# A gated-slot attention kernel: the next unit's scan and reciprocal moved ahead on VectorE, three quantisation steps moved behind the multiplications by the gate

## The chip, the cores and the metric

The kernel runs on one core of one Trainium2 chip. The metric is the device time of one execution in microseconds (us). TensorE is called PE, VectorE DVE, ScalarE ACT, GpSimd POOL and SyncE SP, as the profile calls them.

## What is computed

Four sequences of 512 tokens with 512 features pass a layer of gated slot attention with 16 heads and then a gated feed-forward layer whose weights are rounded to an 8-bit floating-point format. Cut to what the change touches:

```
q, k, v, s, g = LN(x) @ (Wq, Wk, Wv, Ws, Wg)      # per head: 64, 64, 128, 64, 128 wide
z = cumlogsumexp(clip(s, -32, 32)) over tokens    # gate g_t = exp(z[t-1]-z[t]), p = exp(s-z)
hk = hk*g_t + k_t p_t ;  ok = q_t . hk            # scan over tokens
pv = softmax(ok)
hv = hv*g_t + p_t v_t ;  ov = pv . hv             # scan over tokens
o  = ov * rsqrt(mean(ov^2)+eps) * g_norm * silu(g)
x  = x + o @ Wo
x  = x + down(silu(gate(LN(x))) * up(LN(x)))      # weights quantised to fp8
```

In the kernel e is exp(clip(s)), and the running sum of e over the tokens, inverted, is called c: the scan and the reciprocal of the change's name compute it. Both products with hk and hv are done in four chunks of 128 tokens with masked score matrices.

## The kernel before, in words

Work is cut into 32 units: 8 pairs of heads, and in each pair the 4 sequences. A unit u runs the attention of one pair on one sequence; while it does, PE also makes the projections of unit u+1 (`nu`, `ni` in the code). These projections are seven jobs in the order ST (slot logits s), KTJ (k), QT (q) and VG0 to VG3 (v and g of one chunk of 128 tokens each), of twelve 512-column multiplications each, since every operand is split in a high and a low part. The jobs write two PSUM banks in turn, so a job starts only when the job two before it has been drained: VG3 waits for VG1's bank, and ST, the first job of the unit after, waits for VG2's (`job` and `wait_drained`, L371 to L411).

A VG job is drained by two engines. ACT copies v out and takes tanh of half of g (L656, L660); DVE then forms (tanh+1)*g in `gate(c, u, i)` (L885 to L890), and its semaphore `s_g` is what PE waits for. The tanh tile is single: ACT's next tanh waits for DVE's gate on the one before.

Units 0 to 28 are written as one unit and a loop over seven pairs of four units; the last three units are the tail, in which the layer norm of the feed-forward layer is begun (`norm_tokens`, `norm_lo`, and on PE `norm_transposes`, L566 to L574). In the units before the tail DVE also rounds one slice of the feed-forward weights in eight steps (`quantise`, L990 to L1009); SP loads a slice into the tile q8 and stores it when the eighth step is done.

There is no scheduler: the order on each engine is the order in which `unit` of that engine's block is written, and semaphores join the engines. The change is in `unit` of the DVE block (L1011 to L1086), from L1066 on. There, for unit u, DVE goes through:

- `gate(0)` of the next unit; `mask_value_weights(u)` (L901), for which PE's product at L544 waits; `mask_scores(nu)` (L892)
- in the tail `norm_tokens` of two tiles; then `gate(1)` of the next unit
- the last three quantisation steps, L1001 to L1003 (not in the tail)
- `times_gate(u, i, 1)` (L938), `sums(nu, ni)` (L877: a scan at L880, a reciprocal at L883), `times_gate(u, i, 0)`
- in the tail `norm_lo` and `norm_tokens` of the other tiles; then `gate(2)` and `gate(3)` of the next unit

On PE the same stretch holds, in order: the product of masked weights and values (L544), in the tail two tiles' transposes, the jobs VG2 and VG3, in the tail two more tiles' transposes, then in the next unit the transposes of k (L448) and of e (L453), and its job ST. `sums` itself waits only for the exponentials of the next unit (`s_e`), and its result is first read in the next unit at L1034.

Of the kernel before, what the change touches and what calls it, by code (L numbers as in the profile page):

```python
# [145 lines left out]
def attention(nc, sb_top, sem, x, Wq, Wk, Wv, Wg, Ws, Wo, gnorm, flat, gate_s, up_s, fp8_scratch, shared):  # L146
# [3 lines left out]
    with ExitStack() as ctx:  # L150
# [101 lines left out]
        def job_bank(j, i):  # L252

            at = HEAD_JOBS.index(j) if i == 0 else STEADY_JOBS.index(j)
            return PJ[(JOBS * i + at) % 2]
# [603 lines left out]
        def _(dve):  # L859
# [5 lines left out]
            def lo_vg(pair, k):  # L865

                dve.wait_ge(s_vgh, pair * KT + k + 1)
                lo(vgl[:, k, :], stage_vg[:, k, :], vgh[:, k, :]).then_inc(s_vgl, 1)

            def clip(u, i):  # L870
                dve.wait_ge(s_job, job_count(ST, u, i))
                if not isinstance(u, int) or u >= 2:
                    dve.wait_ge(s_b, u - 1)
                dve.tensor_scalar(eT[i % 2][:, :], job_bank(ST, i)[:, :], -CLAMP, CLAMP,  # L874
                                  ALU.max, ALU.min).then_inc(s_clip, 1)

            def sums(u, i):  # L877

                dve.wait_ge(s_e, u + 1)
                dve.tensor_tensor_scan(cT[i % 2][:, :], eT[i % 2][:, :], eT[i % 2][:, :], 0.0, ALU.add,  # L880
                                       ALU.bypass).then_inc(s_scan, 1)
                dve.wait_ge(s_scan, u + 1)
                dve.reciprocal(cT[i % 2][:, :], cT[i % 2][:, :]).then_inc(s_cinv, 1)  # L883

            def gate(c, u, i):  # L885

                dve.wait_ge(s_th, u * CH + c + 1)
                dve.scalar_tensor_tensor(out=g[i % 2][:, c, :, :].rearrange("p a d -> p (a d)"), in0=th[:, :], scalar=1.0,  # L888
                                         in1=job_bank(VGS[c], i)[:, 2 * DV:4 * DV],
                                         op0=ALU.add, op1=ALU.mult).then_inc(s_g, 1)  # L890
# [18 lines left out]
            def key_states(u):  # L909

                dve.wait_ge(s_hkd, u + 1)
                if not (isinstance(u, int) and u == 0):
                    dve.wait_ge(s_ok, u)
                for a in range(2):
                    rows, cols = slice(64 * a, 64 * (a + 1)), slice(M * a, M * (a + 1))
                    dve.tensor_copy(hk[rows, :, cols],
                                    O[0][rows, 0:(CH - 1) * M].rearrange("p (s m) -> p s m", m=M)).then_inc(s_hk, 1)
# [14 lines left out]
            def mean_square(u):  # L932
                dve.wait_ge(s_sq, 8 * (u + 1))
                dve.wait_ge(s_es, u + 1)
                dve.scalar_tensor_tensor(out=ssq[:, :], in0=ssq[:, :], scalar=1.0 / DV, in1=es[:, :],  # L935
                                         op0=ALU.mult, op1=ALU.add).then_inc(s_ms, 1)

            def times_gate(u, i, a):  # L938

                if a:  # L940
                    dve.wait_ge(s_o, 2 * (u + 1))
                    if not (isinstance(u, int) and u == 0):
                        dve.wait_ge(s_tro, 2 * u)
                else:
                    dve.wait_ge(s_sq, 8 * u + CH)
                dve.tensor_tensor(o[:, a, :, :], O[a][:, :].rearrange("p (c d) -> p c d", c=CH),
                                  g[i % 2][:, :, a, :], ALU.mult).then_inc(s_oev, 1)

            def out_norm(u):
                dve.wait_ge(s_rstd, u + 1)  # L950
                dve.wait_ge(s_oev, 2 * (u + 1))
                for a in range(2):
                    scale = rstd[:, :].rearrange("p (c a) -> p c a", a=2)[:, :, a:a + 1].broadcast_to([P, CH, DV])
                    dve.tensor_tensor(o[:, a, :, :], o[:, a, :, :], scale, ALU.mult).then_inc(s_og, 1)

            def out_lo(u, banks):
                for a in range(2):
                    dve.wait_ge(s_oh, 2 * u + a + 1)
                    lo(ol[:, a, :], banks[a][:, :], oh[:, a, :]).then_inc(s_ol, 1)
# [22 lines left out]
            def norm_lo(b, tiles):  # L982
                for c in tiles:
                    t = CH * b + c
                    dve.wait_ge(s_nh, t + 1)
                    cols = slice(t * P, (t + 1) * P)
                    lo(xl[:, :, cols], A[c % 2][:, :].rearrange("p (k t) -> p k t", k=KT), xh[:, :, cols]
                       ).then_inc(s_nl, 1)
# [22 lines left out]
            def unit(u, i, last=False, tail=False):  # L1011
                first = isinstance(u, int) and u == 0
                nu, ni = u + 1, i + 1
                if tail and i >= 2:
                    norm_lo(i - 2, (2, 3))
                if not first:
                    mean_square(u - 1)
                if not last:
                    clip(nu, ni)
                if not first:  # L1020
                    out_norm(u - 1)
                key_states(u)
                value_states(u)
                if not first:
                    out_lo(u - 1, A)
                if i == 3 and not tail:
                    for k in range(2):
                        lo_vg(h_of[0] + 1, k)

                dve.wait_ge(s_ok, u + 1)  # L1030
                dve.wait_ge(s_cinv, u + 1)
                if not first:
                    dve.wait_ge(s_trw, u)
                dve.scalar_tensor_tensor(out=p[:, :].rearrange("p (n t) -> p n t", n=2), in0=ok_both, scalar=SCALE,  # L1034
                                         in1=cT[i % 2][:, :].rearrange("p (n t) -> p n t", n=2),
                                         op0=ALU.mult, op1=ALU.mult).then_inc(s_oks, 1)
                if not first:
                    add_y(u - 1, i - 1, 0)
                    add_y(u - 1, i - 1, 1)

                p3, ok3 = (s[:, :].rearrange("p (s m) -> p s m", m=M) for s in (p, T0))
                dve.wait_ge(s_trs, u + 1)
                dve.tensor_reduce(mx[:, :], ok3, AX.X, ALU.max).then_inc(s_max, 1)
                dve.wait_ge(s_max, u + 1)
                dve.tensor_tensor(p3, ok3, mx[:, :].rearrange("p (s a) -> p s a", a=1).broadcast_to([P, 2 * CH, M]),  # L1045
                                  ALU.subtract).then_inc(s_sub, 1)
                if not first:
                    add_y(u - 1, i - 1, 2)
                    add_y(u - 1, i - 1, 3)
                dve.wait_ge(s_exp, u + 1)  # L1050
                dve.tensor_reduce(sm[:, :], p3, AX.X, ALU.add).then_inc(s_sum, 1)
                if tail:
                    norm_statistics(i - 1)
                else:
                    quantise(u, slice(0, 2))
                dve.wait_ge(s_sum, u + 1)
                dve.scalar_tensor_tensor(out=es[:, :], in0=sm[:, :], scalar=EPS, in1=sm[:, :],
                                         op0=ALU.mult, op1=ALU.mult).then_inc(s_es, 1)

                dve.wait_ge(s_trw, u + 1)  # L1060
                if not first:
                    dve.wait_ge(s_oi, u)
                dve.tensor_tensor(wT[:, :], T1[:, :], cT[i % 2][:, :], ALU.mult).then_inc(s_wT, 1)
                if not tail:
                    quantise(u, slice(2, 5))
                if not last:  # L1066
                    gate(0, nu, ni)
                mask_value_weights(u, i)
                if not last:
                    mask_scores(nu, ni)  # L1070
                if tail:
                    norm_tokens(i - 1, (0, 1))
                if not last:
                    gate(1, nu, ni)
                if not tail:
                    quantise(u, slice(5, Q8_STEPS))
                times_gate(u, i, 1)
                if not last:
                    sums(nu, ni)
                times_gate(u, i, 0)  # L1080
                if tail:
                    norm_lo(i - 1, (0, 1))
                    norm_tokens(i - 1, (2, 3))
                if not last:
                    gate(2, nu, ni)
                    gate(3, nu, ni)  # L1086
# [295 lines left out]
```

## Time and profile before

| what | us |
|---|---|
| median of three runs | 1505.59 |
| lowest and highest run | 1503.77, 1508.01 |
| the profiled execution, its own time | 1505.37 |
| its span, first to last instruction | 1503.7 |
| PE busy | 1431.0 (95%) |
| DVE busy | 1006.4 (67%) |
| ACT busy | 433.3 (29%) |
| POOL busy | 144.3 (10%) |

The profile is of one execution. A unit takes about 36.7 us, the head ends at some 42 us, the attention units at some 1217 us, and the feed-forward layer takes the rest. The granted TensorE clock is 0.992 of full speed in the mean. Busy times of PE overlap at their ends: a 512-column multiplication is shown as 0.39 us long though the next begins 0.23 us after it.

### The profile page before, as it was taken

The page shows a single profiled execution, that of the slowest core. Times are in us where ns is not written, and L with a number is a line of the kernel's source. Part 1 is how long each engine was busy: PE and PEld are TensorE (multiplying, and loading weights), DVE is VectorE, ACT ScalarE, POOL GpSimd, SP SyncE. Part 2 cuts the span into 40 slices and gives each one's busy share as a digit, 9 for nine tenths or more (in the row PEclk, how much of TensorE's full clock was granted, in tenths as well). Part 3 has the DMA queues.
Part 4 walks back from the last instruction along what each step waited for, and adds up shares of the span by engine and source line. Part 5 has one row for each costly group of instructions (what it writes and reads, how often), then busy time and mean ns, then how long its engine had stood idle before and what let it go on. Part 6 is the DMA issues. An engine that isn't in the chain of part 4 may idle for free. (4 is left out here: it accounts for less than half of the span.)

```text
span 1503.7 us, 23604 instructions
## 1 busy us (share of the span) xinstructions
PE 1431.0 (95%) x8480; PEld 1172.0 (78%) x8480; DVE 1006.4 (67%) x1619; ACT 433.3 (29%) x1243; POOL 144.3 (10%) x106
## 2 busy tenths in 40 slices
PE   7899999999999999999999999999999879999998
PEld 6777777777777787778777878787777758888886
DVE  8677776777677777776767776767677764535354
ACT  4323332333223323332323232323232222222221
POOL 3001110111011101110101110111010000000000
PEclk9999999999999999999999999999999989999999
DMA  5011002101110101020102100210000113000000
GB/s 168 20 58 39 22 23 62 39 18 37 42 39 18 50 29 39 18 60 25 32 18 60 31 26 18 61 32 25 18 17 1 57 57 146 29 0 28 0 29 28
DMA packets 61019, 57.23 MB, mean 38 GB/s; under 512 B 7297, under 2 KB 50049, under 8 KB 60929
## 3 DMA queue, kind: packets, MB, share of 16 engines
q1 hardware_dynamic: 60928, 55.87, 11.9%
q8 instruction: 76, 1.25, 0.4%
q14 instruction: 15, 0.11, 0.0%
HBM read 42.22 MB, written 13.63 MB: 37 GB/s over the span
## 5 line engine op out<-in xcount | busy, mean ns | idle before, releaser
L360 PE MATMUL bank<-wvg_hi,xT_hi 128*128 128x512 f32 x512 | 208.8, 408 | 0.0
L362 PE MATMUL bank<-wvg_hi,xT_lo 128*128 128x512 f32 x512 | 200.5, 392 | 0.0
L361 PE MATMUL bank<-wvg_lo,xT_hi 128*128 128x512 f32 x512 | 200.1, 391 | 0.0
L613 ACT ACTIVATE a_and_v<-bank 128x256 f32<-128x256 f32 x128 | 49.0, 383 | 294.4 <-PE bank L362 294.4
L964 DVE TENSOR_TENSOR y<-y,bank 128x512 f32<-128x512 f32 x128 | 87.7, 685 | 66.0 <-PE bank L362 65.8
L888 DVE SCALAR_TENSOR_TENSOR g<-tanh_half_g,bank 128x256 f32<-128x256 f32 x128 | 53.3, 417 | 94.2 <-ACT tanh_half_g L660 94.2
L832 POOL TENSOR_TENSOR rstd<-ssq,neg_half 128x8 f32<-128x8 f32 x32 | 52.4, 1636 | 656.3 <-DVE ssq L935 656.3
L360 PEld LDWEIGHTS bank<-wvg_hi,xT_hi 128*128 128x128 f32 x512 | 96.5, 188 | 21.3 <-issue 0.4
L362 PEld LDWEIGHTS bank<-wvg_hi,xT_lo 128*128 128x128 f32 x512 | 96.2, 188 | 20.8
L361 PEld LDWEIGHTS bank<-wvg_lo,xT_hi 128*128 128x128 f32 x512 | 96.6, 189 | 17.4
L360 PE MATMUL bank<-wo_hi,oT_hi 128*128 128x512 f32 x256 | 107.0, 418 | 1.5 <-DVE oT_lo L863 1.5
L883 DVE RECIPROCAL cT<-cT 128x512 f32<-128x512 f32 x32 | 107.3, 3353 | 1.1
L362 PE MATMUL bank<-wo_hi,oT_lo 128*128 128x512 f32 x256 | 101.3, 396 | 0.0
L361 PE MATMUL bank<-wo_lo,oT_hi 128*128 128x512 f32 x256 | 100.3, 392 | 0.0
L1306 DVE SCALAR_TENSOR_TENSOR gated<-tanh_half,bank 128x512 f32<-128x512 f32 x48 | 32.9, 686 | 100.3 <-ACT tanh_half L1274 100.3
L360 PE MATMUL bank<-xT_hi,ws_hi 128*128 128x512 f32 x128 | 55.0, 430 | 36.8 <-issue 24.9
L1260 PE MATMUL bank<-w_down,fuse_hi 128*128 128x512 f32 x192 | 75.6, 394 | 0.1
L1260 PE MATMUL bank<-w_down,fuse_lo 128*128 128x512 f32 x192 | 75.4, 393 | 0.0
L874 DVE TENSOR_SCALAR eT<-bank 128x512 f32<-128x512 f32 x32 | 22.1, 692 | 71.7 <-PE bank L362 71.7
L1274 ACT ACTIVATE tanh_half<-bank,gate_scale 128x512 f32<-128x512 f32 x48 | 33.1, 689 | 120.8 <-PE bank L119 108.6
L718 ACT ACTIVATE p<-p 128x512 f32<-128x512 f32 x32 | 20.3, 633 | 152.7 <-DVE p L1045 152.7
L544 PEld LDWEIGHTS bank<-a_and_v 128*128 128x128 f32 x512 | 62.1, 192 | 2.7
(157 smaller groups left out, 3215.5 us busy)
## 6 DMA issues: line engine op xcount, KB each, us to landing
fp_weights<-q SPq DMA_DIRECT2D x28, 318.0 KB, 2.6
stage_vg<-in_L_attn_Wv SPq DMA_DIRECT2D x32, 128.0 KB, 2.7
stage_vg<-in_L_attn_Wg SPq DMA_DIRECT2D x32, 128.0 KB, 3.2
stage<-in_L_attn_Wo SPq DMA_DIRECT2D x16, 256.0 KB, 2.7
out<-result SPq DMA_DIRECT2D x16, 256.0 KB, 2.1
y<-in_L_attn_hidden_states SPq DMA_DIRECT2D x3, 1024.0 KB, 9.0
w_down<-fp_weights SPq DMA_DIRECT2D x3, 1024.0 KB, 12.0
q<-in_L_ffn_gate_w SPq DMA_DIRECT2D x28, 106.0 KB, 2.0
```

What stands on the lines that cost most here:

```text
L360: pe.matmul(dst, w_hi, m_hi, start=(k == 0), stop=False)
L361: pe.matmul(dst, w_hi, m_lo, start=False, stop=False)
L362: last = pe.matmul(dst, w_lo, m_hi, start=False, stop=(k == n - 1))
L544: mm = pe.matmul(O[a][:, c * P:(c + 1) * P], av[par][:, a, c, 0, :], av[par][:, a, c, 1, :], start=False, stop=(c == CH - 1), skip_group_c ...
L613: return act.activation(dst, src, ACT.Copy)
L832: pool.tensor_tensor(rstd[:, :], ssq[:, :], neg_half[:, :], ALU.pow).then_inc(s_rstd, 1)
L883: dve.reciprocal(cT[i % 2][:, :], cT[i % 2][:, :]).then_inc(s_cinv, 1)
L888: dve.scalar_tensor_tensor(out=g[i % 2][:, c, :, :].rearrange("p a d -> p (a d)"), in0=th[:, :], scalar=1.0, in1=job_bank(VGS[c], i)[:, 2 ...
L964: dve.tensor_tensor(y[:, t, :], y[:, t, :], out_bank(u, c)[:, :], ALU.add).then_inc(s_ya, 1)
L1260: mm = pe.matmul(Y[c][:, :], part[:, f % 2, c * P:(c + 1) * P], wd[:, f, :], start=(f == 0 and part is fh), stop=(f == FT - 1 and part is fl))
L1274: act.activation(th[:, f % 2, :], gate_up_bank(bank, f, 0)[:, :], ACT.Tanh, scale=hgs[:, f:f + 1]).then_inc(s_th, 1)
L1306: dve.scalar_tensor_tensor(out=ga[:, f % 2, :], in0=th[:, f % 2, :], scalar=1.0, in1=gate_up_bank(bank, f, 0)[:, :], op0=ALU.add, op1=ALU.mult
```

## The change

In DVE's unit, `sums` of the next unit now stands directly in front of `gate(1)`, and the two `times_gate` stand directly behind that gate, ahead of the last three quantisation steps. No instruction is added or removed, and no other engine's order changes.

```diff
                 if tail:
                     norm_tokens(i - 1, (0, 1))
                 if not last:
+                    sums(nu, ni)
                     gate(1, nu, ni)
+                times_gate(u, i, 1)
+                times_gate(u, i, 0)
                 if not tail:
                     quantise(u, slice(5, Q8_STEPS))
-                times_gate(u, i, 1)
-                if not last:
-                    sums(nu, ni)
-                times_gate(u, i, 0)
                 if tail:
                     norm_lo(i - 1, (0, 1))
                     norm_tokens(i - 1, (2, 3))
```

On DVE, in unit 0, from the second of the two masked scores (L898) to the gates of VG2 and VG3; the loop's units have the same order with register instructions between. L888 is `gate`, L1001 to L1003 the last quantisation steps, L946 `times_gate`, L880 and L883 scan and reciprocal. Before:

```order
L898 TENSOR_TENSOR a_and_v<-bank,tri 128x4x128
L888 SCALAR_TENSOR_TENSOR g<-tanh_half_g,bank 128x256 [waits tanh_ready]
L1001 TENSOR_SCALAR q8t<-q8t 128x3x208 [waits fp8_step]
L1002 TENSOR_SCALAR q8t<-q8t 128x3x208 [waits fp8_step]
L1003 SCALAR_TENSOR_TENSOR q<-q8t,q 128x3x208 [waits fp8_step]
L946 TENSOR_TENSOR o<-bank,g 128x512 [waits o_done]
L880 SCALAR_TENSOR_TENSOR cT<-eT 128x512 [waits e_ready]
L883 RECIPROCAL cT<-cT 128x512 [waits c_summed]
L946 TENSOR_TENSOR o<-bank,g 128x512 [waits o_squared]
L888 SCALAR_TENSOR_TENSOR g<-tanh_half_g,bank 128x256 [waits tanh_ready] x2
```

With the change:

```order
L898 TENSOR_TENSOR a_and_v<-bank,tri 128x4x128
L880 SCALAR_TENSOR_TENSOR cT<-eT 128x512 [waits e_ready]
L883 RECIPROCAL cT<-cT 128x512 [waits c_summed]
L888 SCALAR_TENSOR_TENSOR g<-tanh_half_g,bank 128x256 [waits tanh_ready]
L946 TENSOR_TENSOR o<-bank,g 128x512 [waits o_done]
L946 TENSOR_TENSOR o<-bank,g 128x512 [waits o_squared]
L1001 TENSOR_SCALAR q8t<-q8t 128x3x208 [waits fp8_step]
L1002 TENSOR_SCALAR q8t<-q8t 128x3x208 [waits fp8_step]
L1003 SCALAR_TENSOR_TENSOR q<-q8t,q 128x3x208 [waits fp8_step]
L888 SCALAR_TENSOR_TENSOR g<-tanh_half_g,bank 128x256 [waits tanh_ready] x2
```

Scan and reciprocal have moved ahead of the gate of VG1 and of three quantisation steps; the gate of VG2 still follows the same eight instructions.

On DVE in the tail, in unit 30 (unit 29 reads the same but for one wait fewer), from the second `norm_tokens` tile (L979) on; L863 is `norm_lo`. Before:

```order
L979 TENSOR_SCALAR q8t<-y,q8t 128x512 [waits n_transposed]
L888 SCALAR_TENSOR_TENSOR g<-tanh_half_g,bank 128x256 [waits tanh_ready]
L946 TENSOR_TENSOR o<-bank,g 128x512 [waits o_transposed,o_done]
L880 SCALAR_TENSOR_TENSOR cT<-eT 128x512 [waits e_ready]
L883 RECIPROCAL cT<-cT 128x512 [waits c_summed]
L946 TENSOR_TENSOR o<-bank,g 128x512 [waits o_squared]
L863 TENSOR_TENSOR xT_lo<-bank,xT_hi 128x4x128 [waits nT_hi_ready] x2
L979 TENSOR_SCALAR q<-y,q8t 128x512 [waits n_transposed,ln_sd_ready]
L979 TENSOR_SCALAR q8t<-y,q8t 128x512 [waits n_transposed]
```

With the change:

```order
L979 TENSOR_SCALAR q8t<-y,q8t 128x512 [waits n_transposed]
L880 SCALAR_TENSOR_TENSOR cT<-eT 128x512 [waits e_ready]
L883 RECIPROCAL cT<-cT 128x512 [waits c_summed]
L888 SCALAR_TENSOR_TENSOR g<-tanh_half_g,bank 128x256 [waits tanh_ready]
L946 TENSOR_TENSOR o<-bank,g 128x512 [waits o_transposed,o_done]
L946 TENSOR_TENSOR o<-bank,g 128x512 [waits o_squared]
L863 TENSOR_TENSOR xT_lo<-bank,xT_hi 128x4x128 [waits nT_hi_ready] x2
L979 TENSOR_SCALAR q<-y,q8t 128x512 [waits n_transposed,ln_sd_ready]
L979 TENSOR_SCALAR q8t<-y,q8t 128x512 [waits n_transposed]
```

Here too scan and reciprocal stand in front of the gate of VG1; what follows them keeps its order.

## Rows read from the trace of the kernel before

**Rows 1.** The page's busy times of each engine.

```profile
PE 1431.0 (95%) x8480; PEld 1172.0 (78%) x8480; DVE 1006.4 (67%) x1619; ACT 433.3 (29%) x1243; POOL 144.3 (10%) x106
```

**Rows 2.** Groups by form, PE: line, engine, names, shapes, count, busy, mean, idle before.

```profile
L360 PE MATMUL bank<-xT_hi,ws_hi 128*128 128x512 f32 x128 | 55.0, 430 | 36.8 <-issue 24.9 <-DVE g L888 10.3 <-DVE xT_lo L863 1.5
```

**Rows 3.** Timeline of PE, end of unit 12: start, us, engine, line, names, [idle before].

```profile
516.14 0.39 PE L360 MATMUL bank<-wvg_hi,xT_hi 128*128 128x512 f32 x1
...
519.19 0.60 PE L453 MATMUL bank<-ident,eT 128*128 128x128 f32 x4
521.22 0.48 PE L360 MATMUL bank<-xT_hi,ws_hi 128*128 128x512 f32 x1 [1.43 <-issue]
...
524.18 0.88 PE L466 MATMUL bank<-e_tok,k_tok_then_wT 128*64 128x192 f32 x12
```

**Rows 4.** Timeline of DVE, the same stretch.

```profile
509.00 1.27 DVE L898 TENSOR_TENSOR a_and_v<-bank,tri 128x512 f32<-128x512 f32 x2
512.61 0.42 DVE L888 SCALAR_TENSOR_TENSOR g<-tanh_half_g,bank 128x256 f32<-128x256 f32 x1 [2.34 <-ACT tanh_half_g L660]
512.95 0.79 DVE L1001 TENSOR_SCALAR q8t<-q8t 128x636 f32<-128x636 f32 x1
...
515.04 0.68 DVE L946 TENSOR_TENSOR o<-bank,g 128x512 f32<-128x512 f32 x1
515.64 1.22 DVE L880 TENSOR_TENSOR_SCAN cT<-eT 128x512 f32<-128x512 f32 x1
516.89 3.35 DVE L883 RECIPROCAL cT<-cT 128x512 f32<-128x512 f32 x1
520.16 0.63 DVE L946 TENSOR_TENSOR o<-bank,g 128x512 f32<-128x512 f32 x1
520.71 0.41 DVE L888 SCALAR_TENSOR_TENSOR g<-tanh_half_g,bank 128x256 f32<-128x256 f32 x1
```

**Rows 5.** Timeline of ACT, the same stretch: tanh of VG2.

```profile
516.62 0.38 ACT L660 ACTIVATE tanh_half_g<-bank 128x256 f32<-128x256 f32 x1
```

**Rows 6.** Timeline of PE, tail, unit 29.

```profile
1143.54 0.39 PE L362 MATMUL bank<-wvg_hi,xT_lo 128*128 128x512 f32 x1
1145.18 0.63 PE L572 MATMUL bank<-ident,q 128*128 128x128 f32 x4 [1.26 <-DVE q L979]
...
1146.41 0.60 PE L453 MATMUL bank<-ident,eT 128*128 128x128 f32 x4
1146.77 0.48 PE L360 MATMUL bank<-xT_hi,ws_hi 128*128 128x512 f32 x1
```

**Rows 7.** Timeline of DVE, tail, unit 29.

```profile
1134.57 0.54 DVE L979 TENSOR_SCALAR q8t<-y,q8t 128x512 f32<-128x512 f32 x1
...
1143.31 1.27 DVE L863 TENSOR_TENSOR xT_lo<-bank,xT_hi 128x512 fp32r<-128x512 f32 x2
```

**Rows 8.** A stretch at the end of unit 8: busy time of each engine, granted clock (PEclk), DMA.

```profile
373.00:376.00 3.00, 2.77 (x9) 2.26 (x10) 0.71 (x3) 1.36 (x3) 1.60 (x1) 0.73 0.79 216
```

**Rows 9.** Timeline of PE: ST behind units 8 and 24, L466 behind unit 8.

```profile
373.23 0.47 PE L360 MATMUL bank<-xT_hi,ws_hi 128*128 128x512 f32 x1 [1.94 <-issue]
...
377.62 0.95 PE L466 MATMUL bank<-e_tok,k_tok_then_wT 128*64 128x192 f32 x12
...
961.94 0.47 PE L360 MATMUL bank<-xT_hi,ws_hi 128*128 128x512 f32 x1 [2.24 <-issue]
```

**Rows 10.** Single lines, durations in ns min/median/max: reciprocal; one quantisation step.

```profile
L883 DVE RECIPROCAL cT<-cT x32: 3353/3353/3353, 42.1 to 1178.0; 128x512 f32<-128x512 f32 x32
...
L1000 DVE TENSOR_TENSOR q8t<-q x29: 809/821/1781, 66.3 to 1093.0; 128x636 f32<-128x636 f32 x28, 128x624 f32<-128x624 f32 x1
```

**Rows 11.** Timeline of POOL, the same stretch as rows 3 to 5.

```profile
512.12 1.28 POOL L793 TENSOR_TENSOR wo_lo<-stage,wo_hi 128x512 fp32r<-128x512 f32 x1 [5.25 <-ACT wo_hi L613]
```

**Rows 12.** Timeline of DVE, unit 13: its first quantisation step.

```profile
538.28 0.48 DVE L996 TENSOR_SCALAR q8t<-q 128x636 int32<-128x636 int32 x1
```

**Rows 13.** The page's DMA issues: names, queue, count, KB, us to landing.

```profile
fp_weights<-q SPq DMA_DIRECT2D x28, 318.0 KB, 2.6
```

## The prediction

> **What bounds the kernel now.** I read the page's busy times first: PE works 1431.0 of 1503.7 us, DVE 1006.4 [rows 1]. So DVE's work as such is free, and the change can only act through places where PE stands still. The second view groups PE's instructions by form and gives the idle time in front of each. One group holds half of all that is missing: 36.8 us in front of the job ST, of which 1.5 us lie in the head [rows 2]. The other 35.3 us are 29 waits of 0.7 to 2.2 us, one behind each of the units 0 to 28; I take that count from the timeline, where rows 3 and 9 show three of them. The profile puts most of them down to "issue", so the third step is to see in the timelines what they end with. ST starts at 521.22 [rows 3]. ST needs VG2's bank, which is free when DVE's gate of VG2 is done: that gate runs from 520.71 for 0.41, to 521.12 [rows 4]. The wait ends 0.10 us behind it. So the gate of VG2 is what PE waits for, and the question is what keeps it: its tanh was ready at 516.62 + 0.38 = 517.00 [rows 5]. DVE came 3.7 us later, because it had worked without a break since 512.61. Before that it had stood still for 2.34 us, waiting for the tanh of VG1 [rows 4]. The reader is to see both: an idle stretch, then a queue that runs late, on an engine that is idle a third of the time.
>
> **The scan and the reciprocal.** They need only the exponentials of the next unit, which that unit's ACT work made early in unit 12, long before. They can run in the idle stretch. On DVE an instruction starts about 0.08 us before the end shown for the one ahead, so I take start-to-start times [rows 4]: scan 516.89 - 515.64 = 1.25, reciprocal 520.16 - 516.89 = 3.27, gate 512.95 - 512.61 = 0.34, first multiplication by the gate 515.64 - 515.04 = 0.60, second 520.71 - 520.16 = 0.55, three quantisation steps 515.04 - 512.95 = 2.09. The masked scores end at 509.00 + 1.27 = 510.27, so in the new order: scan 510.19, reciprocal 511.44, gate of VG1 at 514.71 to 515.13. That is 2.1 us later than before. Who waits for this gate? ACT's tanh of VG2, not due before 516.62 [rows 5], and PE's job VG3, which starts at 516.14 [rows 3]. A margin of 1.0 us is left, and it is the narrowest place of the change. The move costs nothing while this holds.
>
> **The two multiplications.** They follow at 515.05 and 515.65. The first needs PE's product L544 and ran at 515.04 before, without idle time ahead of it [rows 4], so it is where it was. The second needs the squares of head 0 too, which ACT makes directly behind L544, and before it tanh of VG2 at 516.62 [rows 5]; should they come as late as that, the multiplication would slip by 1 us, and the gate of VG2 by 0.2 us past its margin below. I take no slip. ACT's squares of head 1 need the first alone.
>
> **The quantisation steps.** They run at 516.20, 517.03 and 517.56, to 518.29. What they feed is SP's store of the slice and, through it, the load of the next one. It was finished at about 515.1, now 518.4, 3.3 us later. The store lands 2.6 us after issue [rows 13]; the three loads of 106 KB are smaller than that store, so I bound them by another 2.6. That makes some 523.6, against 538.28 for the first step that reads them [rows 12], or 536.6 once the unit is shorter. The other loads in SP's queue behind this store are bounded by the same shift, and feed splits a unit later. Cover of 13 us: cost zero. If it were gone, each us over it would delay DVE's L1063 and with it PE.
>
> **The gate of VG2, and the gain.** It follows at 518.29 and ends at 518.71. PE could take ST as soon as the transposes of e are issued. What that would be without a wait is seen in the tail: transposes at 1146.41, ST at 1146.77, 0.36 us on [rows 6]. In unit 12: 519.19 + 0.36 = 519.55. The gate is 0.8 us ahead of that. So the wait goes wholly, and 521.22 - 519.55 = 1.67 us are won here. This is 0.24 more than the 1.43 shown as idle, since the profile's ends of pipelined multiplications overlap. For all 29: 35.3 + 29 x 0.24 = **42.3 us**. The waits longer than the usual (2.24 us behind unit 24 [rows 9]) come from a later tanh of VG1, and the new order covers that too: the tanh may come 2.1 us later than in unit 12 before it matters.
>
> **What is late next.** Once ST starts earlier, the stretch from ST to the next unit's masked scores moves with it, since DVE's clip, the transposes and all else there hang on PE. Beside it run the tanh of VG3 and ACT's copies of k and e, which L466 needs 2.96 us after ST [rows 3]. The tanh of VG3 waited for the gate of VG2 too, so it moves up with it. I find nothing that stays behind, and price this at zero, with the first rival for the case that something does.
>
> **The tail.** In units 29 and 30 there is no quantisation. The second norm tile of L979 ends at 1134.57 + 0.54 = 1135.11; scan, reciprocal, gate and two multiplications give 1135.03, 1136.28, 1139.55, 1139.89, 1140.49, then `norm_lo` at 1141.04. It ran at 1143.31 [rows 7]; it lasts 1.27 - 0.08 = 1.19, and the norm tile for which PE waited ends at 1142.23 + 0.54 = 1142.77. PE reaches L572 about 0.22 us after the start of VG3's last multiplication, at 1143.76, and waited until 1145.18 [rows 6]. Won: 1.4 us, in two units **2.8 us**. Unit 31 has neither scan nor quantisation and stays.
>
> **The clock.** Behind unit 8, after PE's wait of 1.94 us, the granted clock is 0.73 in the mean [rows 8], so part of the job ran at 1.2 GHz; ST to L466 took 377.62 - 373.23 = 4.39 us [rows 9] against 2.96 behind unit 12. The longer wait behind unit 24 had no such fall. Without these waits I expect no fall in the units, and take **1.4 us** for it; the bounds are 0 (another place falls instead) and 1.4. The Trainium skill's "TensorE: Matmul & The Clock Gate", section "Part 1: The HAM clock gate", says that the clock is halved unless the engine is kept busy, and that where the change falls varies from run to run; the trace agrees as far as one of 29 waits goes.
>
> **A price beside POOL.** In unit 12 POOL works from 512.12 to 513.40 [rows 11], where the first quantisation step took 0.79; an L1000 took 1.781 us at most against 0.821 in the middle [rows 10], so DVE can be slowed. In the new order the reciprocal lies there, in every fourth unit. It was 3.353 all 32 times [rows 10], but I cannot tell from the trace whether it ever ran beside such work. Bounds: 0 and the 0.96 us of L1000. With 0.96 the gate of VG1 ends 1.0 us before VG3 less 0.96, still in time, and the gate of VG2 comes 0.2 us late in 8 units: 1.6 us. I take 0, as the reciprocal reads one tensor. The skill's "VectorE: DVE Perf Modes", section "Two Vector instructions with no wait between them", says that the read path shared with GpSimd is the one that a second input or a 2-port mode uses; by it the reciprocal is free of POOL, and the sum would be the same 0 where L1000's row alone would give 1.6.
>
> **The sum.** 42.3 + 2.8 + 1.4 = 46.5 us off the profiled execution's 1505.4: **1458.9 us**. That execution stands 0.2 us under the median of the runs, so this is a median too. About 0.3% of 1505, 4.5 us, is what a measurement can tell from no change.
>
> **Rivals.**
> - A new wait takes part of it. PE arrives 1.7 us earlier at L466 and at the output transposes, and the chain gate of VG3, mean square, POOL's power, normalisation might be what then ends last. For it: this chain runs over three engines. Against: its first link moves up with the tanh. If half of the 42.3 is given back, 1458.9 + 21 = 1480 us. 11 in 100.
> - The change does not reach the wait. If "issue" were the sequencer's own time, as the label says for most of it, ST would start when it did: 1505 us. Against: the end of the gate and ST's start lie 0.10 us apart. 4 in 100.
> - Slower: the gate of VG1 becomes VG3's wait. Its place is the first multiplication of VG3. It bites once the gate ends over 1.0 us later than I work out, and outweighs the 1.45 us won per unit from 2.45 us on. If the reciprocal took twice its time in its new place, 3.35 more, VG3 would be 2.4 us late, and 29 x (2.4 - 1.45) = 28 us would be lost: 1533 us. Against: 32 equal durations. With smaller mishaps of the same kind, 5 in 100.
> - The forecast: 80 in 100. Its own range is 1456 (tail and clock give 2 to 3 us more) to 1463 (no gain from the clock, POOL's 1.6, a pair of small waits).
>
> **How the numbers follow.** The range goes up into the first rival, to a fourth or a third given back, 1473, and 1 us under the forecast's own low end, 1455. Faster by over 0.3%: the forecast and the first rival, 0.91. Within 0.3%: the second, 0.04. Slower: 0.05.
>
> **What would show it.** In the profile after: in the group of ST, idle near zero but for the head's 1.5; on DVE no idle before the gate of VG1, which starts where the reciprocal ends, about 3.1 us after the start of L544; gate of VG2 ended before PE's transposes of e are through; VG3 still without a wait; units of 35.3 us instead of 36.7; L572 in the tail without its 1.26. The granted clock stays at 1.00 in the units. The prediction is wrong if PE's idle time turns up before L466, L431 or VG3, or if the waits before ST stay.

## The result, and the profile after

The changed kernel takes 1460.63 us (median of four runs, 1458.88 to 1463.23) against 1504.72 us before. The ratio is 0.9705, with a 95% interval of 0.9683 to 0.9726: 3% faster, by some 44 us. The prediction was 1458.9 us. The profiled execution is the slowest of the four, 1463.23 us with a span of 1461.5; the profiled one of before took 1505.37 with a span of 1503.7.

First the page's busy times after, which answer to [rows 1]; then the group of ST's first multiplications by form, which answers to [rows 2].

```profile
PE 1424.2 (97%) x8480; PEld 1171.4 (80%) x8480; DVE 1001.0 (68%) x1619; ACT 430.3 (29%) x1243; POOL 145.2 (10%) x106
```

```profile
L360 PE MATMUL bank<-xT_hi,ws_hi 128*128 128x512 f32 x128 | 54.0, 422 | 1.5 <-DVE xT_lo L863 1.5
```

The 36.8 us in front of ST have become 1.5, which are those of the head. The timeline shows how, at the end of the same unit 12, which began its L544 (the product of masked weights and values) at 493.30 here and at 511.62 before. DVE, after (before: [rows 4]):

```profile
491.85 1.21 DVE L880 TENSOR_TENSOR_SCAN cT<-eT 128x512 f32<-128x512 f32 x1
493.09 3.35 DVE L883 RECIPROCAL cT<-cT 128x512 f32<-128x512 f32 x1
496.36 0.36 DVE L888 SCALAR_TENSOR_TENSOR g<-tanh_half_g,bank 128x256 f32<-128x256 f32 x1
496.64 1.27 DVE L946 TENSOR_TENSOR o<-bank,g 128x512 f32<-128x512 f32 x2
497.83 0.48 DVE L1001 TENSOR_SCALAR q8t<-q8t 128x636 f32<-128x636 f32 x1
...
499.61 0.41 DVE L888 SCALAR_TENSOR_TENSOR g<-tanh_half_g,bank 128x256 f32<-128x256 f32 x1
501.42 0.42 DVE L888 SCALAR_TENSOR_TENSOR g<-tanh_half_g,bank 128x256 f32<-128x256 f32 x1 [1.40 <-ACT tanh_half_g L660]
```

And PE, after, in the same stretch (before: [rows 3]):

```profile
493.30 1.95 PE L544 MATMUL bank<-a_and_v 128*128 128x128 f32 x16
...
497.81 0.39 PE L360 MATMUL bank<-wvg_hi,xT_hi 128*128 128x512 f32 x1
...
500.92 0.60 PE L453 MATMUL bank<-ident,eT 128*128 128x128 f32 x4
501.27 0.48 PE L360 MATMUL bank<-xT_hi,ws_hi 128*128 128x512 f32 x1
```

No idle time stands in front of the gate of VG1 any more. It starts 3.06 us behind the start of L544 and ends at 496.72, 1.09 us ahead of VG3, which starts at 497.81. The gate of VG2 ends at 500.02, and ST follows the transposes of e after 0.35 us without a wait. DVE's idle time has moved to the gate of VG3, where nobody is kept by it.

In the tail the waits of 1.26 us are gone. These are the second pairs of transposes in units 29 and 30 (before: [rows 6]); the third wait of the kind, in unit 31, stays, as forecast:

```profile
1100.95 0.60 PE L572 MATMUL bank<-ident,q 128*128 128x128 f32 x4
...
1138.03 0.60 PE L572 MATMUL bank<-ident,q 128*128 128x128 f32 x4
...
1171.46 0.63 PE L572 MATMUL bank<-ident,q 128*128 128x128 f32 x4 [0.42 <-DVE q L979]
```

What did not come as forecast is the clock in the tail. Three stretches of it, with busy times of PE, PEld, DVE, ACT and POOL, granted clock, DMA share and GB/s:

```profile
1144.00:1149.00 5.00, 4.07 (x15) 3.64 (x16) 3.98 (x9) 1.19 (x2) 0.06 (x1) 0.66 0.32 119
...
1162.00:1166.00 4.00, 4.00 (x25) 3.32 (x22) 2.20 (x4) 0.00 (x0) 0.00 (x0) 0.57 0.00 0
...
1177.00:1184.00 7.00, 6.49 (x18) 5.20 (x19) 2.13 (x4) 0.00 (x0) 0.00 (x0) 0.60 0.01 4
```

The first two places, the output product of L477 and L431 and the last unit's scores, ran at full clock before; the third was at half clock before too:

```profile
1190.00:1195.00 5.00, 4.40 (x26) 3.84 (x27) 4.42 (x10) 1.14 (x2) 0.00 (x0) 1.00 0.02 5
...
1205.00:1209.00 4.00, 3.73 (x37) 3.26 (x38) 2.42 (x5) 0.00 (x0) 0.64 (x1) 1.00 0.00 0
...
1217.00:1224.00 7.00, 5.11 (x16) 4.09 (x17) 2.54 (x5) 1.19 (x2) 0.00 (x0) 0.54 0.00 1
```

### The profile page after: what moved, and what is told of

Read it like the earlier page. It is cut to its first block and busy times, and to the rows that moved or that the text cites. A ratio compares the mean times of both kernels' runs of the same rounds, so it can differ in the third digit from the quotient of the medians.

```text
span 1461.5 us, 23604 instructions
## 1 busy us (share of the span) xinstructions
PE 1424.2 (97%) x8480; PEld 1171.4 (80%) x8480; DVE 1001.0 (68%) x1619; ACT 430.3 (29%) x1243; POOL 145.2 (10%) x106
## 5 line engine op out<-in xcount | busy, mean ns | idle before, releaser
L361 PE MATMUL bank<-wvg_lo,xT_hi 128*128 128x512 f32 x512 | 200.0, 391 | 0.0
L361 PEld LDWEIGHTS bank<-wvg_lo,xT_hi 128*128 128x128 f32 x512 | 96.5, 189 | 17.3
L883 DVE RECIPROCAL cT<-cT 128x512 f32<-128x512 f32 x32 | 107.3, 3353 | 1.1
L361 PE MATMUL bank<-wo_lo,oT_hi 128*128 128x512 f32 x256 | 100.8, 394 | 0.0
L888 DVE SCALAR_TENSOR_TENSOR g<-tanh_half_g,bank 128x256 f32<-128x256 f32 x128 | 51.6, 403 | 52.5 <-ACT tanh_half_g L660 52.5
L544 PEld LDWEIGHTS bank<-a_and_v 128*128 128x128 f32 x512 | 62.1, 192 | 2.7
L544 PE MATMUL bank<-a_and_v 128*128 128x128 f32 x512 | 62.3, 275 | 0.0
```

The lines of the kernel that those rows point to most:

```text
L361: pe.matmul(dst, w_hi, m_lo, start=False, stop=False)
L544: mm = pe.matmul(O[a][:, c * P:(c + 1) * P], av[par][:, a, c, 0, :], av[par][:, a, c, 1, :], start=False, stop=(c == CH - 1), skip_group_c ...
```

## The experiments

The kernel before was measured again beside each group of experiments, on the same chip, and each ratio is to that time. Its median was 1506.33 us beside the first three and the first of the faster versions, 1507.26 beside the two with added work, and 1506.93 beside the changed kernel's repeat, the one on the loop's head and the second of the faster versions.

### Which of the two moves wins: scan and reciprocal alone

```diff
                 if not last:
                     sums(nu, ni)
                     gate(1, nu, ni)
-                times_gate(u, i, 1)
-                times_gate(u, i, 0)
                 if not tail:
                     quantise(u, slice(5, Q8_STEPS))
+                times_gate(u, i, 1)
+                times_gate(u, i, 0)
```

(against the changed kernel)

> Only the scan and the reciprocal are moved ahead of the gate of VG1; the three quantisation steps stay between that gate and the multiplications. My theory (PE waits for the end of the gate of VG2, and it moves up because scan and reciprocal fill DVE's idle time): the gate of VG2 follows the same eight instructions, so the time is that of the whole change, 1460.6 us within 3. Rival (the multiplications by the gate had to come earlier, or the steps had to move): less of the gain, 1470 us or more, with idle time in front of ST.

Measured: 1462.37 us, ratio to before 0.9702 [0.9682, 0.9722]. The changed kernel, measured again, took 1462.39 us, ratio 0.9704 [0.9688, 0.9720]. The group of ST has the same 1.5 us. So moving scan and reciprocal is the whole gain, and moving the quantisation steps on top of it changes nothing.

### The quantisation steps alone

```diff
                 if not last:
                     gate(1, nu, ni)
-                if not tail:
-                    quantise(u, slice(5, Q8_STEPS))
                 times_gate(u, i, 1)
                 if not last:
                     sums(nu, ni)
                 times_gate(u, i, 0)
+                if not tail:
+                    quantise(u, slice(5, Q8_STEPS))
```

(against the kernel before)

> Only the three quantisation steps are moved, behind the two multiplications; scan and reciprocal stay between these. My theory: the gate of VG2 still ends behind all eight instructions, which start after the idle time, so nothing is won: 1504.7 us within 3, and 35 us of idle time in front of ST. Rival (the order of steps and multiplications carries part of the gain): under 1495 us.

Measured: 1529.54 us, ratio 1.0157 [1.0134, 1.0180], 23 us slower than before; I had expected no change. Groups by form of this kernel, PE and DVE:

```profile
L360 PE MATMUL bank<-xT_hi,ws_hi 128*128 128x512 f32 x128 | 56.4, 441 | 55.3 <-issue 37.7 <-DVE g L888 16.1 <-DVE xT_lo L863 1.5
```

```profile
L946 DVE TENSOR_TENSOR o<-bank,g 128x512 f32<-128x512 f32 x64 | 42.2, 661 | 20.0 <-PE bank L544 19.9
```

The expectation left out that the first multiplication by the gate needs PE's L544. The steps used to fill that time. Without them DVE reaches the multiplication 0.67 us too early in most units and stands still, 20.0 us in all, where the group has 3.6 us in the kernel before. The gate of VG2 is later by that much: 55.3 us in front of ST instead of 36.8. The rest of the 23 us goes with the clock, which fell in five of the units (512-column multiplications of 0.63 us, from 80.4, 305.7, 606.3, 756.5 and 981.7 on) and in one (unit 8) in the kernel before, behind waits that now last 1.9 to 2.0 us at these five places. So the second half of the change would be a loss without the first. With it the multiplications come 1.4 us after L544's results, and the steps need not fill anything.

### Only the end of the gate of VG2

```diff
                 if not last:
                     gate(1, nu, ni)
-                if not tail:
-                    quantise(u, slice(5, Q8_STEPS))
                 times_gate(u, i, 1)
...
                 if not last:
                     gate(2, nu, ni)
                     gate(3, nu, ni)
+                if not tail:
+                    quantise(u, slice(5, Q8_STEPS))
```

(against the kernel before)

> The order of before, but the three quantisation steps stand behind the gate of VG3, so the gate of VG2 ends 1.8 us earlier though scan and reciprocal stay where they were. My theory (only the end of the gate of VG2 counts): it ends before PE's transposes are through (7.3 against 7.9 us behind the start of L544), so nearly all of the gain appears: 1461 to 1468 us, the upper end if the mean square, 1.8 us later, makes the output transposes wait. Rival (the gain needs the scan in DVE's idle time): about 1504 us.

Measured: 1471.56 us, ratio 0.9767 [0.9747, 0.9788]: 34.8 us faster, 3.6 above the upper end of what I expected. Scan and reciprocal are where they were, and yet four fifths of the gain are there, so it is the end of the gate of VG2 that counts and not the place of the scan. The missing fifth, 9.2 us against the 1462.37 of scan and reciprocal alone, has three parts in the traces. The first is the same L544: DVE waits 21.8 us for it here, so that the gate of VG2 starts 7.65 us behind the start of L544 and ends at 8.06, where I had expected 7.3, just past PE's 7.93. ST starts at 8.16, in seven units at 8.43: 22 x 0.23 + 7 x 0.50 = 8.6 us. The second is the tail, where scan and reciprocal stand in their old place and both waits of 1.26 us are back: from unit 29's L544 to unit 31's pass 73.4 us here and 70.5 with scan and reciprocal alone, 2.9 us. The third goes the other way: with scan and reciprocal alone PE loses 3.1 us that it does not lose here, 2.2 at the loop's head and 0.9 in front of unit 0's VG3 (both are taken up below). From unit 0's L544 to unit 29's it is therefore 1029.9 against 1024.2 us, 5.7 more, and with the tail 8.6. In the view of groups the 8.6 us in front of ST hardly show; of the 3.3, 1.5 are the head's:

```profile
L360 PE MATMUL bank<-xT_hi,ws_hi 128*128 128x512 f32 x128 | 54.2, 423 | 3.3 <-issue 1.8 <-DVE xT_lo L863 1.5
```

The 0.24 us per wait that the overlapped ends hide are the larger part here: 6.8 of 8.6 us.

### The margin: more work in front of the gate of VG1

```diff
                     sums(nu, ni)
+                    dve.reciprocal(pad[:, 0:N], eT[ni % 2][:, 0:N])
                     gate(1, nu, ni)
```

(against the changed kernel, with N = 96 and N = 384; `pad` is a new tile that nobody reads)

> The whole change, and in front of the gate of VG1 one more reciprocal on DVE, of 96 columns into a tile that nobody reads: some 0.65 us by the 3.35 us of 512 columns. My theory of the margin: the gate of VG1 ends 1.0 us and the gate of VG2 1.1 us before PE needs them, so the addition is free: 1461 us within 3. Rival (DVE bounds the unit in the new order): 31 x 0.65 = 20 us more, 1481 us.

> The same with a reciprocal of 384 columns, about 2.45 us from start to start. My theory: the gate of VG1 now ends 1.45 us behind the moment at which PE could start VG3, in each of 31 units, and the gate of VG2 just before its own: 45 us more, about 1506 us, and the idle time stands in front of VG3, not of ST. Rival one (DVE bounds): 31 x 2.45 = 76 us more, 1537 us. Rival two (PE's queue hides it): under 1475 us.

Measured: 1465.73 us with 96 columns (ratio 0.9729 [0.9713, 0.9745]) and 1517.13 us with 384 (1.0073 [1.0056, 1.0090]). Who waited for whom on PE, of the kernel with 384 columns (us in total, times, longest; its lines are one higher, so L361 is the first line of `product3`, L449 the transposes of k, L889 the gate):

```profile
PE bank L361 <- DVE g L889: 40.0, 31, 2.0
...
PE bank L449 <- issue: 5.9, 6, 1.1
```

The forecast wait is there, 31 times, once per unit, at one place:

```profile
523.29 0.47 PE L361 MATMUL bank<-wvg_hi,xT_hi 128*128 128x512 f32 x1 [1.31 <-DVE g L889]
```

1.31 us shown plus what overlap hides is about the 1.45 us expected: a unit inside a pass of the loop lasts 36.7 us from L544 to L544, where the changed kernel takes 35.21, so 1.5 us; 31 of them are 46. ST has no wait. This turns the rival "the gate of VG1 becomes VG3's wait" into something seen: it bites from about 1 us of added work (2.45 us added less the 1.5 lost), and with 2.45 us added the kernel is slower than the one before. The total is 11 us above what I expected. Most of it stands in the units from L544 to L544. The six that reach over a jump back of the loop are 1.1 to 1.4 us longer than the others, 7.7 us in all, where the changed kernel's repeat has 1.9. The first lasts 39.0 us, with half clock from 78.6 on. The changed kernel itself takes 1.8 us more in its repeat than the 1460.6 from which I worked. The 1465.73 us with 96 columns are 1.7 above the range that I gave. The gate makes no wait in the loop, only one of 1.1 us in unit 0, but the row of L449 is there too:

```profile
PE bank L449 <- issue: 4.7, 6, 1.0
...
PE bank L361 <- DVE g L889: 1.1, 1, 1.1
```

So 0.7 us more on DVE costs nothing in front of VG3 and ST in the steady units. What the kernel has over the changed one, 3.3 us, lies mostly elsewhere: at the first instruction of the loop's body PE stood still in six of seven passes, each time that it had jumped back.

### The loop's head

In the changed kernel PE's transposes of k also wait at the loop's head, 0.7 us in three of seven passes, and in the kernel before 0.28 once. In the kernel with 96 columns SP's store of the quantised slice is issued at 220.90, 0.96 us ahead of such a wait at 221.86.

```diff
-                if not tail:
-                    quantise(u, slice(5, Q8_STEPS))
...
                 if not last:
                     gate(2, nu, ni)
                     gate(3, nu, ni)
+                if not tail:
+                    quantise(u, slice(5, Q8_STEPS))
```

(against the kernel with 96 columns added)

> The kernel with the added reciprocal of 96 columns showed PE idle at the first instruction of the loop's body (the transposes of k), in six of the seven passes, 4.7 us in all, put down to issue. There SP's store of the quantised slice starts 1 us ahead of that instruction. Here the last three quantisation steps stand behind the gate of VG3, so that the store starts 3 us later, behind the loop's head; one more reciprocal stays. Theory (the store's transfer delays PE's first instruction after the jump back): that idle time goes, under 1 us is left, and the time is 1461 to 1466 us, the rest from the mean square coming later. Rival (the longer program delays it, wherever the store lies): 4 to 5 us of idle time stay there.

Measured: 1466.82 us, ratio 0.9736 [0.9720, 0.9752]. The row that decides, who waited for whom on PE:

```profile
PE bank L449 <- issue: 3.8, 6, 0.9
```

The store is now issued at 223.63, 2.2 us behind the instruction that waited at 221.44, and the wait stays. My theory of the store is refuted.

The traces say more. Each has an instruction queue (q8, kind "instruction") beside the data queue, and at every jump back one 16 KB packet of it lands shortly before PE's transposes of k. It is this one in the kernel with 96 columns, behind unit 8, where L449 starts at 363.86 after 0.98 us of idle time (queue, kind: packets, MB, share, window 361.0 to 362.5):

```profile
q8 instruction: 1, 0.02, 3.9%
```

It ran from 361.37 to 362.29, and L449 started 1.6 us behind its end. All eleven traces together have 66 jumps back. In the 38 where PE is shown idle there, the transposes start 1.51 to 1.62 us behind the end of the packet, though the packets last from 0.9 to 1.8 us; in the 28 others they start 1.52 to 2.01 us behind it, never sooner. And the packet's own start follows the gate of VG1, for which PE waits last ahead of the jump, in front of VG3:

| kernel | gate of VG1 ends | packet starts | PE idle shown at the head |
|---|---|---|---|
| before | 1.3 to 2.2 | 4.3 | 0.28 us, once |
| changed | 3.4 | 4.7 to 5.0 | 0.7 us |
| with 96 columns | 4.0 | 5.3 to 5.9 | 4.7 us |
| with 384 columns | 5.85 | 7.1 to 7.6 | 5.9 us |

(us behind the start of L544, over the six jumps back of each trace.) In the eight kernels in which scan and reciprocal stand ahead of that gate the packet starts 1.3 us behind the gate's end in 36 of 48 cases, and up to 1.9 us in the others; the two kernels with added work move the gate and the packet moves with it. So the reading that fits all 66 is that PE waits at the loop's head for instructions, and that these are fetched later when the gate of VG1 ends later. It is a second place, besides VG3, where that gate costs time, and at the changed kernel's 3.4 us its margin is already used up. No kernel without the jump was run, and why the packet starts 0.5 us later in some cases is not shown.

### A faster version: three more waits of the same kind

```diff
-            sums(0, 0)
             dve.wait_ge(s_const, 4)
             mask_scores(0, 0)
             gate(B - 1, 0, 0)
+            sums(0, 0)
...
+                if not first:
+                    mean_square(u - 1)
                 if tail and i >= 2:
                     norm_lo(i - 2, (2, 3))
-                if not first:
-                    mean_square(u - 1)
...
-                if tail:
+                if tail and not last:
                     norm_statistics(i - 1)
-                else:
+                elif not tail:
                     quantise(u, slice(0, 2))
...
                 dve.tensor_tensor(wT[:, :], T1[:, :], cT[i % 2][:, :], ALU.mult).then_inc(s_wT, 1)
+                if last:
+                    norm_statistics(i - 1)
```

(against the changed kernel)

> The whole change and three more reorderings on DVE: in the head the scan and the reciprocal behind the masked scores and the gate of VG3; in the tail the mean square ahead of the leftover norm tiles; in the last unit the layer-norm statistics behind L1063. Each takes work from in front of something PE waits for: 3.3 us (L448 in the head), 2.0 us (L431 in unit 31) and 2.75 us (L527 in unit 31). My theory, that each wait ends with the DVE instruction named and nothing else is as late: 8 us off 1460.6, 1452.6 us, up to 3 us less where a fall of the clock behind a wait goes too. Rival: the next wait is as late, and under 3 us are won.

> The kernel with the three reorderings in head and tail, and of the change only the scan and reciprocal moved (the quantisation steps again ahead of the multiplications by the gate), so the store starts 1.2 us earlier, at 5.2 instead of 6.4 us behind the start of L544. My theory: the same time, 1452.3 us within 2. Rival (the place of the quantisation steps matters by itself): over 1455 us.

Measured: 1452.30 us, ratio to before 0.9636 [0.9620, 0.9653], and with the quantisation steps back between the gate of VG1 and the multiplications 1451.61 us, ratio 0.9633 [0.9617, 0.9649]. The second was measured beside the changed kernel's 1462.39: 10.8 us less. Who waited for whom on PE, changed kernel first:

```profile
PE bank L431 <- DVE o L954: 4.2, 2, 2.3
PE bank L448 <- DVE a_and_v L898: 3.3, 1, 3.3
PE bank L527 <- DVE k_tok_then_wT L1063: 2.8, 1, 2.8
```

and the version with all three:

```profile
PE bank L431 <- DVE o L954: 2.3, 1, 2.3
...
PE bank L448 <- DVE a_and_v L898: 0.9, 1, 0.9
```

Two waits are gone; of the head's 3.3 us 0.9 stay. That makes 7.1 of the 10.8 us. Most of the rest is the clock, in two places. Unit 0's L544 starts at 66.80 us in the second version and at 70.24 in the changed kernel's repeat, 3.4 us sooner where 2.4 of the wait went: the half clock there (0.50 from 46 to 49 us in the changed kernel) is gone. The nine other traces all have it, and neither of these two. From unit 30's L544 to unit 31's 28.7 us pass instead of 35.0, 6.3 less where 4.7 of waits went: a stretch at half clock is gone there too. This one cannot be credited to the reordering alone, since the kernel with scan and reciprocal alone has the same waits and no fall there. The two versions, which differ by the place of the quantisation steps alone, agree within 0.7 us, as the first experiment did.

## Why the prediction was right

**What bounds.** The reading held: the idle time in front of ST ended with the gate of VG2, though the profile calls most of it "issue". The experiment on the end of that gate shows it, since another way to bring it forward also wins.

**The gain in the units.** From unit 0's L544 to unit 29's the kernel before takes 1135.65 - 70.55 = 1065.10 us, the changed one 1092.84 - 70.27 = 1022.57. L544 of units 0, 29, 30 and 31, before:

```profile
70.55 1.95 PE L544 MATMUL bank<-a_and_v 128*128 128x128 f32 x16
...
1135.65 1.95 PE L544 MATMUL bank<-a_and_v 128*128 128x128 f32 x16
...
1174.14 1.95 PE L544 MATMUL bank<-a_and_v 128*128 128x128 f32 x16
...
1208.99 1.95 PE L544 MATMUL bank<-a_and_v 128*128 128x128 f32 x16
```

and after:

```profile
70.27 1.95 PE L544 MATMUL bank<-a_and_v 128*128 128x128 f32 x16
...
1092.84 1.95 PE L544 MATMUL bank<-a_and_v 128*128 128x128 f32 x16
...
1129.91 1.95 PE L544 MATMUL bank<-a_and_v 128*128 128x128 f32 x16
...
1166.39 1.95 PE L544 MATMUL bank<-a_and_v 128*128 128x128 f32 x16
```

That is 42.5 us won against 42.3 + 1.4 = 43.7 forecast for waits and clock together. The missing 1.2 us stand at the loop's head. In the changed kernel 24 of the 29 stretches from L544 to L544 last 35.21 us; the five others, 0.1 to 0.5 us longer and 1.4 in all, are each one that reaches over a jump back. Before, such a delay stood there twice (0.4 and 0.1 us), hidden behind the wait for the gate of VG2; the change lets it show, and lengthens it by ending the gate of VG1 later. I had no term for it: "the move costs nothing while this holds" and "I find nothing that stays behind" were wrong by 1.2 us.

**Margins.** The forecast start of the gate of VG1, 3.09 us behind L544's start, came at 3.06. Its margin of 1.0 us was 1.09 in unit 12, and the two kernels with added work show where it ends. But unit 12 is not the narrowest place. In unit 0 the gate of VG1 starts 3.71 us behind L544 and ends 0.45 us ahead of VG3, and in the repeat of the same kernel it is late:

```profile
69.42 1.29 POOL L793 TENSOR_TENSOR wo_lo<-stage,wo_hi 128x512 fp32r<-128x512 f32 x1 [4.12 <-ACT wo_hi L613]
69.46 2.33 DVE L880 TENSOR_TENSOR_SCAN cT<-eT 128x512 f32<-128x512 f32 x1
...
75.60 0.47 PE L360 MATMUL bank<-wvg_hi,xT_hi 128*128 128x512 f32 x1 [0.68 <-DVE g L888]
```

The prediction named idle time before VG3 as a sign of being wrong. It is there once, in unit 0, and costs 0.9 us (36.13 us from unit 0's L544 to unit 1's instead of 35.21).

**The tail.** From unit 29's L544 to unit 30's 38.49 us became 37.07: 1.42 won, the forecast 1.4.

**The clock.** Here a term was mis-sized for the profiled execution. I took 1.4 us for a fall that goes, with "another place falls instead", worth 0, as the other bound; what came is 1.4 won and 3.05 lost, outside both. The fall in unit 8 did go, and no unit of the loop has one in the changed kernel. But from unit 30's L544 to unit 31's 36.48 us passed where 34.85 less 1.42 was due: 3.05 us lost at half clock, behind waits of 1.98 and 2.75 us that both kernels have. In the three other executions of the changed kernel the mean clock was 0.993 or 0.994, not 0.991, and they took 1458.88 to 1460.86 us. In the same place the changed kernel's repeat took 35.0 us, with one stretch at half clock, and the kernel with scan and reciprocal alone 33.4, with none. The order of work there is the same in all three, so the loss belongs to this execution more than to the change. The sentence that the falls vary from run to run (the Trainium skill, "TensorE: Matmul & The Clock Gate", section "Part 1: The HAM clock gate") fits the spread: waits of the same length met full clock in one trace and half clock in the other.

**The sum.** Before unit 0's L544 0.3 us were won, in the units 42.5, in unit 29 1.4; from unit 30's L544 to unit 31's 1.6 were lost, and behind it 0.5. That makes the 42.1 us between the two spans, 4.4 short of the forecast 46.5: 1.2 for the loop's head and some 3 for the clock. The medians are 44.1 us apart, and that the median lies 1.7 us from the forecast, closer than the profiled execution, is in part the chance of where the clock fell.

**POOL.** I took no slowing of the reciprocal beside POOL. It was 3.352 to 3.353 us in all 32 cases of the changed kernel, in unit 12 too, where POOL's subtraction ran from 493.60 for 1.27 us, wholly beside it (from 493.09 for 3.35 us). POOL has such work there in one unit of four; in these the zero is shown. What the bounds left out is the scan, which in unit 0 begins within 0.15 us of POOL's subtraction. In the rows of the repeat above POOL began first, and the scan took 2.33 us instead of its usual 1.21. In the profiled execution the scan began first, and POOL took 2.28 us instead of 1.29:

```profile
69.45 1.22 DVE L880 TENSOR_TENSOR_SCAN cT<-eT 128x512 f32<-128x512 f32 x1
...
69.46 2.28 POOL L793 TENSOR_TENSOR wo_lo<-stage,wo_hi 128x512 fp32r<-128x512 f32 x1 [4.16 <-ACT wo_hi L613]
```

The slowed scan is what makes VG3 wait in unit 0.

**The quantisation steps.** "Cost zero" was right, but for a reason that I had not seen: their old place filled the wait for L544, and only the later gate of VG1 makes them free to go. Moved alone they cost 23 us. The prediction costed the two moves in one sum and could not see this.

## What to carry to other kernels

An engine that is idle a third of the time can still set the pace: look at what its last instruction before a wait of the bound engine had queued ahead of it, and whether an idle stretch lies just ahead of that queue. Work whose inputs are long ready belongs in such a stretch. Before a filler is moved away, ask what it fills, and cost each move of a change by itself. When an instruction is made later, look for everything that waits for it; here that included the instructions behind the loop's jump back.

## What the runs showed of the hardware that was not expected

Idle time in front of the first of a run of multiplications is shown too small by 0.24 us, since their ends overlap in the view: 29 waits are shown as 35.3 us, while from unit 0's L544 to unit 29's the kernel before takes 44.0 us more than 29 x 35.21, of which 1.4 are the clock, so that the waits were worth 42.6; in the third experiment 6.8 of 8.6 us did not show at all.

PE stood still behind the jump back of its loop, up to 1.1 us a pass, more in the kernels with one more instruction on DVE (3.8 to 5.9 us in all, against 0.7), wherever the store of the slice lay. Its first instruction there never started sooner than 1.51 us behind the end of a 16 KB packet of the instruction queue, in 66 jumps back of eleven traces.

The scan on DVE, which is given the same tile twice as its input, and a two-input subtraction on POOL did not run beside each other at full speed. In the eight kernels in which the two begin within 0.15 us of each other in unit 0, the one that began first kept its time. In six the scan began second and took 2.2 to 2.3 us instead of 1.2; in two the subtraction began second and took 2.2 to 2.3 us instead of 1.3. The reciprocal, with one input, kept 3.352 to 3.356 us in all of them.
